# One block's turned tile evacuated bank by bank, and new orders inside the periods of an attention and feed-forward kernel

## What is computed

```python
xn = layernorm(x)                                  # x: 4 x 1024 x 256
q, k, v = xn @ wq + bq, xn @ wk + bk, xn @ wv + bv # 16 query heads, 2 key/value heads of 16
q, k = rotary(q) / 4, rotary(k)
attn = softmax(q @ k.T / 4) @ v                    # per batch and head, 1024 x 1024 scores
ffn = fwht(silu(xn @ W1.T) * (xn @ W3.T)) @ W2.T   # hidden size 1024
out = x + attn @ wo + bo + ffn
```

## Time and profile before

| | us |
|---|---|
| median of 3 timed runs | 1179.03 (1177.75 to 1181.44) |
| profiled execution, its own time | 1181.6 |
| its span, first to last instruction | 1179.8 |
| PE busy | 1049.8 (89%) |
| DVE busy | 783.2 (66%) |
| ACT busy | 704.7 (60%) |
| POOL busy | 352.2 (30%) |
| granted TensorE clock, mean | 0.936 |

### The profile page before, as it was taken

How to read it: one execution, slowest core, us unless ns; L and a number is a source line. 1 busy time by engine, 2 the same in 40 slices (tenths; PEclk the granted TensorE clock), 3 DMA queues, 4 the chain that set the end, 5 groups by cost and what they waited for, 6 DMA issues and landing times.

```text
span 1179.8 us, 19333 instructions
## 1 busy us (share of the span) xinstructions
PE 1049.8 (89%) x7584; PEld 547.5 (46%) x7584; DVE 783.2 (66%) x891; ACT 704.7 (60%) x1318; POOL 352.2 (30%) x299
## 2 busy tenths in 40 slices
PE   0358899989998999989998999989999999999994
PEld 0314354544555455544555445554445344544552
DVE  4895477757776577766777577765777777687611
ACT  2204377656765477655775567754775667656771
POOL 1652523107330254106330164204440023102310
PEclk9755799989999899989999799989999999999997
DMA  8247022412314223412205123421204101410001
GB/s 222 67 150 192 21 67 68 101 59 72 89 31 88 70 82 88 94 63 75 83 13 109 54 99 89 88 69 31 73 20 101 48 24 46 95 36 6 7 17 51
DMA packets 62732, 84.27 MB, mean 71 GB/s; under 512 B 16688, under 2 KB 31920, under 8 KB 62640
## 3 DMA queue, kind: packets, MB, share of 16 engines
q1 hardware_dynamic: 59328, 78.30, 24.8%
q10 hardware_dynamic: 3312, 4.72, 1.6%
HBM read 55.18 MB, written 22.54 MB: 66 GB/s over the span
## 4 chain that ended last, share of the span: by engine, by line
PE 79%; DVE 12%; ACT 3%; issue 2%; ACTq 1%; SPq 1%; DMA 1%; POOL 0%; POOLq 0%; DVEq 0%
PE ps L1387 19%; PE ps L1339 16%; PE ps L1374 15%; PE ps L1297 13%; DVE negpart L1124 9%; PE ps L1352 7%; PE ps L1277 3%; PE ps L1307 3%; ACT work L942 2%; PE ps L1313 1%; ACTq L878 1%; DVE y L1106 1%; PE ps L1302 0%; DVE y L1104 0%; ACT osum L950 0%
## 5 line engine op out<-in xcount | busy, mean ns | idle before, releaser
L1124 DVE TENSOR_REDUCE negpart<-ps 128x2 f32<-128x1024 f32 x512 | 619.3, 1223 | 272.6 <-PE ps L1297 267.7
L942 ACT ACTIVATE work<-ps 128x512 f32<-128x512 f32 x1024 | 552.9, 605 | 266.4 <-PE ps L1374 211.0
L1297 PE MATMUL ps<-kb,qh 48*128 48x512 f32 x1024 | 257.7, 472 | 53.4 <-DVE negpart L1124 27.4
L1374 PE MATMUL ps<-qh,kb 50*128 50x512 f32 x1024 | 272.0, 470 | 20.0 <-ACT work L942 19.3
L1387 PE MATMUL ps<-work,vb 128*32 128x512 f32 x2048 | 282.0, 626 | 0.0
L1374 PEld LDWEIGHTS ps<-qh,kb 50*128 50x128 f32 x1024 | 121.2, 192 | 218.9 <-ACT work L942 166.8
L1339 PE MATMUL ps<-xf,w_p 64*128 64x512 f32 x1536 | 207.1, 401 | 5.9 <-DVE negpart L1124 3.5
L1297 PEld LDWEIGHTS ps<-kb,qh 48*128 48x128 f32 x1024 | 109.2, 197 | 149.0 <-DVE negpart L1124 83.2
L1339 PEld LDWEIGHTS ps<-xf,w_p 64*128 64x128 f32 x1536 | 140.7, 186 | 52.6 <-DVE hid L1096 12.7
L825 POOL TENSOR_TENSOR hid_p<-hid,hid_p 128x512 fp32r<-128x512 f32 x64 | 82.3, 1286 | 196.0 <-ACT hid_p L933 196.0
L831 POOL TENSOR_TENSOR attnt<-attnt,recips 128x512 f32<-128x512 f32 x16 | 20.4, 1278 | 374.6 <-DMA recips<-recip_rows 374.6
(11 more groups left out here) (109 smaller groups left out, 489.0 us busy)
## 6 DMA issues: line engine op xcount, KB each, us to landing
xf<-xn_parts SPq DMA_DIRECT2D x32, 512.0 KB, 7.8
qh<-qk_parts SPq DMA_DIRECT2D x192, 64.0 KB, 2.2
xn_parts<-xt SPq DMA_DIRECT2D x14, 512.0 KB, 3.6
y<-in_x SPq DMA_DIRECT2D x8, 512.0 KB, 4.1
attnt<-osum SPq DMA_DIRECT2D x128, 32.0 KB, 2.0
recips<-recip_rows SPq DMA_DIRECT2D x128, 32.0 KB, 1.8
out<-y SPq DMA_DIRECT2D x8, 512.0 KB, 2.9
xn<-in_x SPq DMA_DIRECT2D x7, 512.0 KB, 4.5
```

Of the source, the lines that this page charges most:

```text
L942: nc.scalar.activation(prob[j % 2][:, h, :], ps[:, 4 + u % 3, :], ACT.Exp, scale=SCALE).then_inc(exp_done, 1)
L1124: nc.vector.tensor_reduce(negpart[a][:, f, :, h, t, e], two(slot), AX.X, ALU.max, negate=True).then_inc(ring_free[slot], 1)
L1297: m = pe.matmul(bank[:, r, :], qh[2 * q + f][rows, h, t * P:(t + 1) * P], kb[i % 2][rows, e * 512:(e + 1) * 512], start=True, stop=True)
L1374: pe.matmul(ps[:, 4 + u % 3, :], kb[i % 2][rows, kt * P:(kt + 1) * P], qh[2 * a + f][rows, h, :], start=True, stop=True).then_inc(s2_done, 1)
```

## The change

The number of matmuls, of scores, sums and pieces stays. Two things change.

**The turned tile.** Its two PSUM banks are announced to ACT one by one (`done = True` after each piece), ACT casts each bank by itself, and DVE subtracts each by itself; in steady state an exponential stands between the two casts.

The core of the diff:

```diff
-FULLS = {"QK": 2}
-FREES = {"UP": 2, "VT": 2}
+FULLS = {"XT": 2, "QK": 2}
+FREES = {"XT": 2, "UP": 2, "VT": 2}
...
-            def turned_hi(m):
+            def turned_hi(m, k):
                 slot = RING[("XT", m)][0]
-                act.wait_ge(*filled(("XT", m)))
-                if m > 1:
+                act.wait_ge(*filled(("XT", m), k + 1))
+                if m > 1 and k == 0:
...
-                nc.scalar.copy(turned_x(m)[0][:, :, :], two(slot)).then_inc(xnt_hi, 1)
+                nc.scalar.copy(turned_x(m)[0][:, k, :], two(slot)[:, k, :]).then_inc(xnt_hi, 1)
...
                     if kind == "UP":
...
                         exponentials(i, j, 1, 4)
+                        gate(i, p - 4)
                         hidden_before(i, p)
-                        gate(i, p - 4)
                         exponentials(i, j, 4, 5)
                         linear(i, p - 4)
...
                     elif kind == "XT":
-                        turned_hi(i + 2)
+                        turned_hi(i + 2, 0)
+                        exponentials(i, j, 0, 1)
+                        turned_hi(i + 2, 1)
+                        exponentials(i, j, 1, 3)
                         save_finished(i, p)
-                        exponentials(i, j, 0, 8)
+                        exponentials(i, j, 3, 8)
...
-            def turned_lo(m):
+            def turned_lo(m, k):
                 slot = RING[("XT", m)][0]
-                dve.wait_ge(xnt_hi, m + 1)
-                nc.vector.tensor_tensor(turned_x(m)[1][:, :, :], two(slot), turned_x(m)[0][:, :, :].bitcast(F32),
+                dve.wait_ge(xnt_hi, DC * m + k + 1)
+                nc.vector.tensor_tensor(turned_x(m)[1][:, k, :], two(slot)[:, k, :], turned_x(m)[0][:, k, :].bitcast(F32),
                                         ALU.subtract).then_inc(ring_free[slot], 1)
...
                     elif kind == "DN":
                         extra_before(i, p)
-                        units(i, u, 3)
+                        units(i, u, 4)
                         down(i, p - 12)
-                        units(i, u + 3, 1)
```

More of the change, by code:

```diff
@@ L144, in walk_iteration @@
         elif kind == "DN":
+            first(0)
             scores(0)
-            first(0)
             first(1)
@@ L155, in walk_iteration @@
             first(1)
-            extra()
             scores(3)
@@ L159, in walk_iteration @@
             sums(i, 2 * p)
+            extra()
         elif kind == "WO":
-            scores(0)
-            first(1)
             extra()
             first(0)
+            first(0)
+            sums_before()
+            first(1)
+            scores(0)
             scores(1)
-            sums_before()
+            own(0, 1, 2, 3)
             scores(2)
             sums(i, 2 * p)
-            own(0, 1)
             first(1)
             scores(3)
-            own(2, 3)
-            first(1)
         elif kind == "W2":
@@ L187, in walk_iteration @@
         elif kind == "XT":
+            first(1)
+            own(0, 1)
+            scores(0)
+            scores(1)
             sums_before()
-            own(0)
-            first(1)
             extra()
[L192 to L195, removed]
+            first(0)
             first(1)
             scores(2)
+            scores(3)
             first(0)
-            scores(3)
             sums(i, 2 * p)
@@ L205, in walk_iteration @@
             scores(1)
+            sums_before()
             scores(2)
+            scores(3)
             first(1)
-            sums_before()
             own(0, 1, 2, 3)
             first(1)
-            scores(3)
+            sums(i, 2 * p)
             extra()
-            sums(i, 2 * p)
         elif kind is None:
@@ L226, in walk_iteration @@
         elif kind == "UPx":
+            scores(0)
             first(0)
-            scores(0)
+            first(1)
             sums_before()
             scores(1)
+            own(0)
+            scores(2)
             first(1)
-            own(0, 1)
+            own(1, 2)
             first(1)
-            own(2, 3)
-            first(1)
-            scores(2)
+            own(3)
             sums(i, 2 * p)
@@ L240, in walk_iteration @@
         elif kind == "DNx":
+            first(1)
             scores(0)
+            own(0)
             scores(1)
-            first(0)
+            own(1)
+            first(1)
             sums_before()
             first(1)
-            own(0, 1)
             scores(2)
-            own(2)
+            own(2, 3)
             first(1)
-            own(3)
+            sums(i, 2 * p)
+            extra()
             scores(3)
-            sums(i, 2 * p)
-            first(0)
-            extra()
         elif kind == "WOx":
@@ L259, in walk_iteration @@
             scores(1)
-            own(1)
+            scores(2)
             first(1)
-            scores(2)
-            own(2, 3)
+            own(1, 2, 3)
             first(1)
@@ L1029, in _ @@
                     elif kind == "WO":
-                        exponentials(i, j, 0, 2)
                         save_finished(i, p)
-                        exponentials(i, j, 2, 8)
+                        exponentials(i, j, 0, 8)
                     elif kind is None:
@@ L1178, in _ @@
             norm_stats(1)
-            turned_lo(0)
-            turned_lo(1)
+            turned_lo(0, 0)
+            turned_lo(0, 1)
+            turned_lo(1, 0)
+            turned_lo(1, 1)
             rotate_queries(dve, nc.vector, 0)
```

67 lines of the change are left out of this document (36 added, 31 removed).

## The result

The changed kernel takes 1165.08 us in the median of four runs (1162.71 to 1169.32), against 1179.0 of the kernel before: ratio 0.9872, interval 0.9848 to 0.9896. It is faster by 14 us, not by 39, and lies above the range.

A forecast was written before the change was run, and what follows sets the result against it. PE was taken to bound the kernel, through its waits and half-clock stretches. Terms 30.5 + 1 + 16 + 2.4 - 8.9 - 2.3 = 38.7 us gave 1142.9 from the profiled 1181.6, or 1140 against 1179.0; range 1131 to 1163.

The forecast's parts named there:

- What bounds the kernel: Whole kernel: PE sets the time; only removing PE waits or stretches at half clock can shorten it.
- XT and QK: Periods of i = 1 to 5: XT 7.2 us, QK 10.2, at full clock; gain 30.5 us.
- DN: DN and DNx periods: earlier max frees slot 1, fewer PE waits; 2.3 us in each of 7 iterations, gain 16.
- UP at no cost: The 48 UP periods: later exponential delays a score by 0.1 us, hidden by another wait; cost 0, bounds 0 and 14.
- The cover that I named, `gated`: UP periods: PE waits for `gated` anyway, 0.25 us later than it could go, so the 0.1 delay vanishes.
- UPx: The 16 UPx periods: from 8.68 to 8.5 us each; gain 2.4 us, between 0 and 6.
- WOx and WO: WOx and the two WO periods: scores calls put together and other waits; losses of 8.9 and 2.3 us.
- my rival on the slower side: Clock also falls in WOx periods, about 3.3 us each; slower from six falls on, 1200 us with 12; chance 0.04.
- The profile against the median: Whole kernel: profiled execution 2.6 us above the timed median, so 1142.9 us became a forecast of 1140.
- The rival that UP loses its cover: All 48 UP periods: PE pays 0.1 to 0.3 us in each; time 1145 to 1155 us; chance 0.1.
- the signs that I had named for being wrong: Mean clock still 0.94, UP periods longer by 0.1 us, or half clock in UP or WOx.

The follow-up runs named there:

- experiment 3: Kernel before with only the split tile and the new XT and QK orders: 1168.03 us, ratio 0.9868.
- experiment 8: Kernel before with the split tile and new XT, QK, DN and DNx orders; UP, UPx, WO and WOx as before: 1144.55 us, ratio 0.9695.
- experiment 4: Kernel before with only the new DN and DNx orders: 1172.97 us, ratio 0.9934.
- experiment 2: Changed kernel with ACT's order of before put back in UP: 1157.84 us, ratio 0.9804.
- experiment 9: Changed kernel with UPx's orders of before, UP's ACT order staying new: 1165.27 us, ratio 0.987.
- experiment 11: Kernel of experiment 8 with WOx's third scores call moved up behind the second: 1166.47 us, ratio 0.9889.
- experiment 1: Changed kernel with the PE, ACT and DVE orders of before put back in WO and WOx: 1148.92 us, ratio 0.973.
- experiment 10: Kernel of experiment 8 with QK's order of before on PE, ACT and DVE: 1139.27 us, ratio 0.9653.
- experiment 12: Kernel of experiment 8 with no two scores calls together in XT and QK, ACT's copy of the sums one exponential earlier: 1138.76 us, ratio 0.9649.

## Why the prediction was wrong, step by step

The direction was right, and so was the mechanism of the largest term; the range was not: measured 1165, low end 1131, high end 1163, point 1140. In the profile 38.7 us were predicted and 18.9 came.

- **What bounds the kernel** was right: PE's waits and the clock. Each of the five falls in XT went with the holes, as forecast; that the holes made them is not shown by that alone.
- **XT and QK: right, 27.7 for 30.5.** XT 7.49 for 7.2, QK 10.45 for 10.2. QK's count was kinder than its own numbers: 15.5 and 15.3 less 5.7 leave 9.8 and 9.6, not 9.1 to 9.7, and the 10.2 starts from the 9.1. I left out that it hangs on DN: by itself the part gives 13.7 us (experiment 3).
- **DN: right in direction, sized too high.** 8.1, or 9.6 without the one fall at p = 12 of i = 7, for 16; with UP's order of before 10.5 (experiment 8), so 5.5 of the shortfall is DN's own. In experiment 4 p = 13 came out better than counted (4.9 for 0.6 x 7), p = 15 gave 5.1 for 0.9 x 7; but DNx lost 0.15 instead of 0.5 each and p = 12 nothing for 0.3 x 7. In DNx two waits of 0.32 and 0.33 for slot 1 stand where one of 0.45 for the pair stood. At p = 12 the wait for slot 1 grew from 0.10 to 0.33 (experiment 4), and the wait of 0.16 for `down`, which I had counted in p = 13, falls ahead of that period's first instruction, so into p = 12. The new UP order adds 0.1 there (experiment 2).
- **UP at no cost: the step that failed in kind.** The cover that I named, `gated`, is there, and p = 7, 8 and 11 indeed cost nothing. But p = 5 and 9 are followed by UPx, which has no such wait of PE at its start. In the changed kernel it begins with scores, and these wait. Timeline of all engines at that boundary of the changed kernel (i = 3; tanh, the last scores but two, cast, exponential, copy, the scores, `gated`, the exponentials, and UPx's first scores):

```profile
547.93 0.60 ACT L919 ACTIVATE hid<-ps 128x512 f32<-128x512 f32 x1 [0.55 <-PE ps L1345]
...
548.16 0.40 PE L1380 MATMUL ps<-qh,kb 50*128 50x512 f32 x2
...
548.43 0.61 ACT L931 CAST hid_p<-hid 128x512 fp32r<-128x512 f32 x1
...
548.93 0.60 ACT L940 ACTIVATE work<-ps 128x512 f32<-128x512 f32 x1
...
549.42 0.59 ACT L927 COPY hid<-ps 128x512 f32<-128x512 f32 x1
...
549.49 0.60 PE L1380 MATMUL ps<-qh,kb 50*128 50x512 f32 x2
549.51 0.68 DVE L1098 SCALAR_TENSOR_TENSOR hid<-hid,ps 128x512 f32<-128x512 f32 x1
...
549.89 1.60 ACT L940 ACTIVATE work<-ps 128x512 f32<-128x512 f32 x3
...
550.57 0.99 PE L1380 MATMUL ps<-qh,kb 50*128 50x512 f32 x2 [0.24 <-ACT work L940]
551.05 0.18 PEld L1380 LDWEIGHTS ps<-qh,kb 50*128 50x128 f32 x1 [0.30 <-ACT work L940]
```

The score that the exponential at 578.27 of the earlier trace rows (p = 7) reads, in the kernel before:

```profile
577.83 0.40 PE L1374 MATMUL ps<-qh,kb 50*128 50x512 f32 x2
```

That exponential started 0.44 after its score; it now starts 0.77 after it (548.93), behind tanh and cast; the three exponentials behind it are 0.3 late (549.89, 1.73 after that score, where it was 1.40 before, 577.83 to 579.23), and the next period's first score stands 0.24 for them. Before, the two periods took together 15.89:

```profile
556.50:564.03 7.53, 7.51 (x56) 3.86 (x56) 5.49 (x5) 5.83 (x12) 3.12 (x3) 1.00 0.44 161
564.03:572.39 8.36, 8.22 (x59) 4.03 (x59) 6.88 (x8) 5.65 (x11) 2.58 (x2) 1.00 0.01 2
```

and now 7.85 + 8.40 = 16.25. I had written both facts down, one as covered, the other inside UPx's count, and had not added the one to the other. The scores at UPx's start are only where the wait shows: with UPx's order of before the loss stands inside UPx (experiment 9). Forecast at 0, UP's order costs 3.8 us and 0.9 in DN p = 12, by experiments 8, 9 and 2.
- **UPx: the sign was wrong.** Forecast was a gain of 2.4; against experiment 8 the order by itself costs 2.1 (experiment 2). I had taken the window of 8.68, which is p = 10 of i = 3, for all 16; the eight p = 6 and three of the p = 10 took 6.97 to 8.38, all but one, before. The new order brings p = 10 of i = 3 to 8.45 and p = 6 to 8.40. The 0.7 gained in the table above is there because part of the loss is counted in p = 5 and 9.
- **WOx and WO: the waits right, the falls not.** Without the three falls (about 1.5 each, by 9.11 and 10.59 for p = 3) WOx costs 7.2 for my 8.9, WO 2.4 for 2.3. The falls add 4.4 that the sum didn't have. The falls were my rival on the slower side, given 0.04. It came true in part: in 3 of 14 WO periods in one profile, in 4 in the next. I had tied it to the XT falls staying, which was needless.
- **The profile against the median.** I took 2.6 off the profiled time for the median. The changed kernel's profiled execution was its fastest and its median 2.4 above. Together that is the 5.0 that stands between 18.9 and 13.9. The slower executions had a mean clock of 0.949 and 0.948 (1166.9 and 1169.3 us), the faster ones 0.952 and 0.953, so the longer ones spent more time at half clock.
- The rival that UP loses its cover came near in size (4.3 for 5 to 15), not in its reason: it had all 48 periods pay, and p = 7, 8 and 11 paid nothing.
- Of the signs that I had named for being wrong two came: UP periods longer by 0.1 and more (p = 5 and 9), and half clock in WOx.

The longest gap of PE in the XT periods of the kernel before, where the clock fell, was 1.67 us, and in experiment 11 it fell in a period without one over 0.45 us. The rule of the Trainium skill ("TensorE: Matmul & The Clock Gate", Part 1, HAM oscillation), which ties the fall to idle gaps longer than any of these, does not explain them: the trace disagrees. The measurement decides.

What stays open is what exactly makes the clock fall. Most falls in WO periods came with the new orders and went with the old ones (experiments 1 and 11), but not all: p = 2 of i = 7 has a fall with WOx's order of before in experiments 8 and 10. It begins at 1017.5 us in experiment 8, and these are PE's only waits in that period:

```profile
1014.98 0.50 PE L1382 MATMUL ps<-qh,kb 50*128 50x512 f32 x1 [0.22 <-ACT work L941]
1015.85 0.50 PE L1304 MATMUL ps<-kb,qh 48*128 48x512 f32 x2 [0.38 <-DVE negpart L1129]
```

The same period of the kernel before has waits of 0.23 and 0.38 and no fall. On the other side WO of i = 6, with waits of 1.32 and 1.02 and busy for 7.31 of 10.10, kept 1.00, and the window at 656.10 with 9.69 of 10.59 lost it. Neither the longest wait nor the idle share tells them apart.

## What to carry to other kernels

When two streams are reordered, list for each period what is late at its end and what the next period asks for first; a wait that is covered inside the period can be paid at the seam, and a part's gain may rest on another part. To price one part, put it on a kernel that has all the others. Where a resource is three deep, two groups of two in a row can cost a wait for the round trip, here from nothing (QK, experiment 12) to 1.2 us (WOx, experiment 11). And a stretch with small waits may cost a multiple of them in clock, in some executions only: look at the spread of the runs and at more than one profile before believing either.

## What the hardware showed that I had not expected

The same instruction stream lost the clock at 660, 906, 1032 and 1111 us in one execution and at 266, 789, 905 and 1038 us in another, in one common period out of seven, with falls of 3.4 to 10.2 us. From i = 1 on, nearly everything between them was equal to 0.05 us. A fall came where PE was busy for 9 tenths of the period (656.10) and stayed away where it was busy for 7 (912.66). The executions of the two kernels without a fall in any WO period and none in XT or QK (experiments 1 and 12) lie within 1.5 and 1.7 us; those of kernels with WO's new orders within 2.9 to 14.3 (experiments 2 and 9).
